# A six-layer perceiver block on one core: constant rows, background units, first keys and the last expert's rows are placed elsewhere

## What is computed

```
x = x + L0 linear cross-attention with ctx (4 x 2048 x 512)
x = x + L0 gated linear attention (128 steps), its output through Wo, plus the row bo
x = x + L0 feed-forward net 512 -> 2048 -> 512 (gelu), plus the row b2
x = x + L1 masked cross-attention with ctx, 16 heads
x = x + L1 causal self-attention with rotary embedding, 16 heads
x = x + L1 mixture of 8 experts, 2 per token (silu(x W1) * (x W3)) W2
```

## Time and profile before

| | |
|---|---|
| median of 3 runs | 1844.7 us (1841.14 to 1847.6) |
| the profiled execution | 1843.16 us |
| its span, first to last instruction | 1841.6 us |
| mean granted TensorE clock | 0.977 of 2.4 GHz |
| busy: PE, DVE, ACT, POOL | 94%, 64%, 53%, 13% |
| instructions | 25720 |

### The profile page before, as it was taken

The page is one execution under the profiler, slowest core; times in us unless marked ns, Lnnn a source line. Parts: engine busy times, 40 slices in busy tenths (PEclk is TensorE's granted clock), DMA queues, the critical chain, the costliest instruction groups (busy, mean ns, idle before and its releaser), DMA issues. The chain is left out here.

```text
span 1841.6 us, 25720 instructions
## 1 busy us (share of the span) xinstructions
PE 1740.0 (94%) x9446; PEld 1428.0 (78%) x9446; DVE 1172.4 (64%) x2453; ACT 982.1 (53%) x2033; POOL 235.9 (13%) x138
## 2 busy tenths in 40 slices
PE   7999999999898989999999999999899879999996
PEld 5778888877787779999899989887455557778785
DVE  5777777764534236667677767998434456785753
ACT  6676666642343235556566656887332345665552
POOL 0000000000000022112111211222111022221221
PEclk9999999999999999999999999999899979999998
DMA  6322222217400599778677867667500347786721
GB/s 227 119 104 86 98 81 102 69 69 286 166 1 23 183 290 301 240 225 248 188 234 220 245 188 221 178 197 246 198 6 7 119 165 249 248 299 208 275 65 59
DMA packets 147131, 310.01 MB, mean 168 GB/s; under 512 B 11472, under 2 KB 100816, under 8 KB 135440
## 3 DMA queue, kind: packets, MB, share of 16 engines
q1 hardware_dynamic: 145072, 301.85, 50.1%
q0 software_dynamic: 1920, 6.36, 1.1%
HBM read 226.88 MB, written 81.28 MB: 167 GB/s over the span
## 5 line engine op out<-in xcount | busy, mean ns | idle before, releaser
L1131 ACT CAST PTH<-bank 128x512 fp32r<-128x512 f32 x256 | 149.8, 585 | 164.9 <-PE bank L1126 164.9
L1133 DVE TENSOR_TENSOR PTL<-bank,PTH 128x512 fp32r<-128x512 f32 x256 | 176.0, 687 | 94.9 <-ACT PTH L1131 93.8
L1652 DVE TENSOR_TENSOR WS<-EW,WS 128x1024 fp32r<-128x1024 f32 (+1 forms) x120 | 148.4, 1244 | 80.9 <-ACT WS L1649 78.9
L1111 ACT ACTIVATE TT<-TT,MX 128x512 f32<-128x512 f32 x256 | 186.5, 729 | 8.6 <-DVE MX L1101 8.6
L1083 DVE CUSTOM_DVE_ANT_0 TT<-bank,MASK 128x512 f32<-128x512 f32 x256 | 174.1, 681 | 5.9 <-POOL MASK L1064 5.3
L1649 ACT CAST WS<-EW 128x1024 fp32r<-128x1024 f32 (+1 forms) x144 | 139.1, 977 | 63.3 <-PE bank L1669 62.5
L1126 PE MATMUL bank<-IDN,TT 128*128 128x128 f32 x1024 | 155.2, 274 | 4.0 <-DVE RS L1176 2.9
L101 PE MATMUL bank<-BCH,WKT 128*128 128x256 f32 x512 | 150.6, 294 | 5.2 <-DVE BCL L633 4.4
L102 PE MATMUL bank<-BCL,WKT 128*128 128x256 f32 x512 | 146.9, 287 | 0.0
L103 PE MATMUL bank<-BCH,WKT 128*128 128x256 f32 x512 | 146.8, 287 | 0.0
L1152 PE MATMUL bank<-PTH,VG 128*128 128x256 f32 x512 | 142.6, 300 | 0.2 <-DVE PTL L1133 0.2
(11 more groups left out here) (293 smaller groups left out, 4352.0 us busy)
## 6 DMA issues: line engine op xcount, KB each, us to landing
EW<-in_ewg SPq DMA_DIRECT2D x48, 1024.0 KB, 5.5
KST<-tmp_k SPq DMA_DIRECT2D x43, 768.0 KB, 5.7
tmp_k<-EKH SPq DMA_DIRECT2D x128, 256.0 KB, 2.8
EW<-in_ewg SPq DMA_DIRECT2D x24, 768.0 KB, 4.8
CT<-in_ctxT SPq DMA_DIRECT2D x32, 512.0 KB, 3.2
CN<-in_ctxN SPq DMA_DIRECT2D x32, 512.0 KB, 3.2
BCT<-in_ctxT SPq DMA_DIRECT2D x32, 512.0 KB, 3.5
tmp_k<-EKL SPq DMA_DIRECT2D x64, 256.0 KB, 2.7
```

Of the source, the lines that this page charges most:

```text
L1111: t_e[(n, kc)] = tick("act", act.activation(TT[:, sl, cs], TT[:, sl, cs], ACT.Exp, bias=MX[:, n % 4, 5:6], scale=SC1, accum_out=SUM[:, b % ...
L1131: t = tick("act", act.copy(PTH[:, q], bank[bk][:]))
L1133: t = free[bk] = tick("dve", dve.tensor_tensor(PTL[:, q], bank[bk][:], f(PTH[:, q]), ALU.subtract))
L1652: t_lo = tick(low, E[low].tensor_tensor(WS[:, s, 1, 0:n * w], src, f(WS[:, s, 0, 0:n * w]), ALU.subtract))
```

## The change

Four edits. (1) `GBO` is added to X of batch b in level b of the gated attention, and `B2R` in step 4 + b of the feed-forward loop. (2) At the end of both layers, the addition of a bank to X, `norm_rate`, and for batches 1 and 2 `norm_rows` of the batch before, stand together in `add_and_rate`, with one unit after each batch; `layernorm_all` begins with the transposes and loses its `bg(4)`. Before the feed-forward net it stands behind the split of the first weights. Before the cross-attention only SP waits ahead of it, and for the work up to the last feed-forward product; ACT and DVE wait for that behind it. (3) The units of batch 0 ahead of the first loads end with its last key tile (`k_done`); `load_head` waits for the keys' stores alone, and the four units left are issued after `load_head(0)`. (4) The last expert's rows are not stored. The selection matrices of its two blocks are turned (`ST`), the higher expert's rows of the other experts are gathered in the last expert behind `LB`, and X + `LB` + `HB` is written into four banks that a product has opened; then the rows' high and low halves (`YH`, `YL`) are added in those banks by products with `ST`. ACT and DVE copy the banks to X, and each batch is stored at once. The count for long lists is loaded in the last expert. The block for lists over 256 tokens makes its own gathers and additions and stores again; it is skipped with these inputs. In the diff the additions of `LB` stand behind the first block's eighth weight group, `open_sum` ahead of the second block's ninth, and `spread_one` is eight products that need the second block's halves and the four opened banks.

```diff
-        def layernorm_all(bg, high=None):
-            t_r = [norm_rate(b) for b in range(4)]
-            t_n = [norm_rows(b, t_r[b]) for b in range(2)] + [None] * 2
-            bg(4)
+        def add_and_rate(b, bk, t_r, t_n):
+            t = tick("dve", dve.tensor_tensor(X[:, b, :], X[:, b, :], bank[bk][:], ALU.add))
+            x_tok[b] = free[bk] = t
+            t_r[b] = norm_rate(b)
+            if 0 < b < 3:
+                t_n[b - 1] = norm_rows(b - 1, t_r[b - 1])
+        def add_row(b, row):
+            need("dve", x_tok[b])
+            x_tok[b] = tick("dve", dve.tensor_tensor(X[:, b, :], X[:, b, :], row, ALU.add))
+        def layernorm_all(bg, t_r, t_n, high=None):
...
+                    if c == 1 and g % 8 == 7:
+                        k_done[b] = list(bgs["kw"])
...
+            if 0 <= lev < 4:
+                add_row(lev, GBO[:])
             bg(2)
...
         for b in range(4):
             need("pe", free[4 + b])
-            t = tick("pe", pe.matmul(bank[4 + b][:], ..., GWO[:], start=True, stop=True))
-            need("dve", t, x_tok[b])
-            t = tick("dve", dve.tensor_tensor(X[:, b, :], X[:, b, :], bank[4 + b][:], ALU.add))
-            free[4 + b] = t
-            need("dve", t)
-            x_tok[b] = tick("dve", dve.tensor_tensor(X[:, b, :], X[:, b, :], GBO[:], ALU.add))
+            t_o.append(tick("pe", pe.matmul(bank[4 + b][:], ..., GWO[:], start=True, stop=True)))
+        for b in range(4):
+            need("dve", t_o[b], x_tok[b])
+            add_and_rate(b, 4 + b, t_r, t_n)
+            bg(1)
...
-        t_yt = layernorm_all(bg, YTH)
...
         split_w1(0)
+        t_yt = layernorm_all(bg, t_r, t_n, YTH)
...
+                if 4 <= i < 8:
+                    add_row(i - 4, B2R[:])
+        fg = so_far()
         for b in range(4):
             need("dve", t_y, x_tok[b])
-            t = tick("dve", dve.tensor_tensor(X[:, b, :], X[:, b, :], bank[4 + b][:], ALU.add))
...
-            x_tok[b] = tick("dve", dve.tensor_tensor(X[:, b, :], X[:, b, :], B2R[:], ALU.add))
+            add_and_rate(b, 4 + b, t_r, t_n)
+            bg(1)
...
-        fg = so_far()
-        for e in ("sp", "act", "dve"):
+        need("sp", *fg)
+        t_yt = layernorm_all(bg, t_r, t_n)
+        for e in ("act", "dve"):
             need(e, *fg)
-        t_yt = layernorm_all(bg)
         bg(2)
...
-        bg_rest()
+        while k_done[0] is None:
+            bg()
...
-                while kv_done[b] is None:
+                while k_done[b] is None:
                     bg()
-                need("sp", *kv_done[b])
+                need("sp", *k_done[b])
...
-        for n in range(NK):
+        load_head(0)
+        bg_rest()
+        for n in range(1, NK):
             load_head(n)
...
+        def out_high(v, bk):
+            T[v]["yh"] = tick(SEM[v]["act"], act.copy(YH[v][:], bank[bk][:]))
+        def out_low(v, bk):
+            T[v]["yl"] = tick(SEM[v]["dve"], dve.tensor_tensor(YL[v][:], bank[bk][:], f(YH[v][:]), ALU.subtract))
+        def turn_list(v):
+            need("pe", free[5], t_c)
+            for i in range(4):
+                m = pe.transpose(bank[5][:, 128 * i:128 * i + 128], f(GS[v][:, i, :]), IDN[:])
...
+            t_st[v] = free[5] = tick("act", act.copy(ST[v][:], bank[5][:].rearrange("p (a b) -> p a b", a=4)))
+        def open_sum(i, bk):
+            need("pe", free[bk], *t_st)
+            t = tick("pe", pe.matmul(bank[bk][:], ST[0][:, i, :], XG[0][:, 0], start=True, stop=True))
+            need("dve", t, t_hb[3], x_tok[i])
+            t_sum[i] = tick("dve", dve.tensor_tensor(bank[bk][:], X[:, i, :], HB[i], ALU.add))
+        def spread(v, i, bk, x, stop):
+            return pe.matmul(bank[bk][:], ST[v][:, i, :], (YH, YL)[x][v][:], start=False, stop=stop, skip_group_check=True)
...
                 if g == 1 and last:
                     for i in range(4):
                         back(i)
+                    for i in range(4):
+                        back_high(i)
+                    for eng in engines:
+                        load_count(eng, 8)
+                if g in (2, 3) and last:
+                    turn_list(g - 2)
...
+            if last:
+                for i in range(4):
+                    need("dve", t_lb[3])
+                    x_tok[i] = tick("dve", dve.tensor_tensor(X[:, i, :], X[:, i, :], LB[i], ALU.add))
...
+            sums = (b, b1, 4, 5)
+            if last:
+                for i in range(4):
+                    open_sum(i, sums[i])
...
+        when("pe", 7, spread_one)
+        out_high(0, a)
+        out_low(0, a)
+        need("pe", T[0]["yh"], *t_sum)
+        for i in range(4):
+            spread(0, i, sums[i], 0, False)
+        need("pe", T[0]["yl"])
+        for i in range(4):
+            t = tick("pe", spread(0, i, sums[i], 1, True))
+            e = ("act", "dve")[i % 2]
+            need(e, t)
+            x_tok[i] = tick(e, (dve.tensor_copy if i % 2 else act.copy)(X[:, i, :], bank[sums[i]][:]))
+            need("sp", x_tok[i])
+            t_out = dma("sp", "out", out[:, i], X[:, i])
...
-        for i in range(4):
-            t = tick("hb", pool.indirect_dma_start(HB[i][:], None, YD, ...))
-        for i in range(4):
-            need("dve", t_lb[3])
-            x_tok[i] = tick("dve", dve.tensor_tensor(X[:, i, :], X[:, i, :], LB[i][:], ALU.add))
-        for i in range(4):
-            need("dve", t_hb, x_tok[i])
-            x_tok[i] = tick("dve", dve.tensor_tensor(X[:, i, :], X[:, i, :], HB[i][:], ALU.add))
-        finish_at(stop)
+        need("sp", t_out, *so_far())
```

More of the change, by code:

```diff
@@ L612, in build @@
         kv_done = [None] * 4
+        k_done = [None] * 4
         def split_weights(dst, src, t):
@@ L1792, in group_one @@
                 when("dve", e, lambda: gate(1, g // 2, bk), ("dve1",))
-            if g == 8:
+            if g == 8 and e < 7:
                 when("act", e, lambda: out_act(1, bk), ("act1",))
                 store(e, 1)
+            if g == 8 and e == 7:
+                when("act", e, lambda: out_high(1, bk), ("act1",))
+                when("dve", e, lambda: out_low(1, bk), ("dve1",))
         def half_zero(e, g, h, bk):
@@ L1925, in build, with spread_one @@
             nxt = half_zero(e, 8, 1, a)
-            out_act(0, a)
-            store(e, 0)
+            if not last:
+                out_act(0, a)
+                store(e, 0)
             split_half(nxt)
-        engines = ("sp", "pe", "act", "dve", "pool")
+        def spread_one():
+            need("pe", T[1]["yh"], T[1]["yl"], *t_sum)
+            for i in range(4):
+                spread(1, i, sums[i], 0, False)
+                spread(1, i, sums[i], 1, False)
+        when("pe", 7, spread_one)
[5 more added lines that the diff above has]
+        need("pe", T[0]["yl"])
+        for i in range(4):
+            t = tick("pe", spread(0, i, sums[i], 1, True))
[4 more added lines that the diff above has]
+            t_out = dma("sp", "out", out[:, i], X[:, i])
         own = {"xsp0": "sp", "xsp1": "sp", "xpe": "pe", "xact": "act", "xdve": "dve"}
@@ L2034, in far_block @@
                 wait(eng, *[(o, P.count[o]) for o in own])
-        fin = [(k, P.count[k]) for k in ("pe", "act", "dve", "pool", "pe1", "peg", "act1", "dve1", "yw0", "yw1", "lb")]
+        fin = [(k, P.count[k]) for k in ("pe", "act", "dve", "pool", "pe1", "peg", "act1", "dve1", "yw0", "yw1", "lb",
+                                         "hb", "out")]
         blocks = {}
@@ L2044, in build, with far_add @@
                 blocks[e, kb] = todo, {o: P.count[o] - before[o] for o in own}
+        FAR = CMP[:, 0, 0:32].rearrange("p (a b) -> p a b", a=4)
+        XF, LF = P.sem_of("xfar"), P.sem_of("xlb")
+        def far_add():
+            steps = [
+                lambda: dve.tensor_scalar(FAR, POS[:], 256.0, None, ALU.is_ge),
+                lambda: dve.tensor_tensor(FAR, FAR, KEY[:], ALU.mult),
+                lambda: dve.tensor_reduce(KFT[:, 0:4], FAR, AX.X, ALU.add),
+                lambda: dve.tensor_reduce(KFT[:, 4:8], FAR, AX.X, ALU.max),
+                lambda: dve.tensor_tensor(KFT[:, 0:4], KFT[:, 0:4], KFT[:, 4:8], ALU.subtract),
+                lambda: dve.tensor_scalar(SM2[:], KFT[:, 0:8], 0.0, None, ALU.is_equal),
+                lambda: dve.tensor_scalar(SM2[:], SM2[:], 3585.0, None, ALU.mult),
+                lambda: dve.tensor_tensor(KFT[:, 0:8], KFT[:, 0:8], SM2[:], ALU.add),
+                lambda: dve.tensor_scalar(FIN[:], KFT[:, 0:8], -1.0, None, ALU.add)]
+            for n, step in enumerate(steps):
+                step().then_inc(XF, 1)
+                dve.wait_ge(XF, n + 1)
+            dve.wait_ge(LF, 128)
+            n = len(steps)
+            for rows in (LB, HB):
+                for i in range(4):
+                    dve.tensor_tensor(X[:, i, :], X[:, i, :], rows[i], ALU.add).then_inc(XF, 1)
+                    n += 1
+                dve.wait_ge(XF, n)
         for eng in engines:
-            need(eng, *fin)
```

(3 more changed lines are left out.)

45 lines of the change are left out of this document (32 added, 13 removed).

## The result

The changed kernel takes **1827.1 us**, the median of 4 runs (1825.0 to 1828.1), beside 1844.4 for the kernel before: a ratio of 0.9906, with a 95% interval of 0.9893 to 0.9919, so 17.3 us less (15 to 20). A second set of runs gave 1825.7 and 0.9903 (0.9889 to 0.9916). The forecast was 1821, a gain of 23.7 on the median shown then; 1827 lies in its range.

What follows compares the result with a forecast made beforehand. TensorE, busy for 94% of the span, was taken as the bound, so only its waits counted. Gains 6.5+4.8-1.1+3.9+8.3 = 22.4 us off the profiled 1843.2 gave 1820.8, stated as 1821, range 1814 to 1829.

Steps and rivals of the forecast that it cites:

- The constant rows: Eight additions (`GBO`, `B2R`), each as long as 0.69 us, leave the chains at both joins for beside products; cost nothing.
- Join 1: Between gated attention and feed-forward net: first feed-forward product 4.7 us sooner, 1.8 less low clock, sum 6.5; 1.4 gap remains.
- The walk: Step-by-step VectorE and TensorE timing between gated attention and feed-forward net: a 1.4 us gap remains, first feed-forward product at 491.5.
- Join 2: After the feed-forward net, up to the query products: gain 4.8 us, with a gap of 1.3 us remaining.
- The two gaps left: Gaps of 1.4 and 1.3 us remaining in the joins: clock charged behind one of the two, 1.1 us.
- Head 0's keys: Before the first score: key load goes out sooner, the gap and its low clock go, 3.9 us (ends 0 and 3.9).
- keys no sooner: Rival before the first score: the load's data come as late as now, gain there 0; 1825 us, chance 0.13.
- the forecast's own signs of being wrong: A gap over 3 us in any join, clock falling where 1.00 now, or TensorE waiting for a last-expert POOL split.
- The tail: Behind the last product: store, four gathers and eight additions removed, products added; 8.3 us gained (ends 5.5 and 10.1).
- The sum: Whole kernel: 6.5+4.8-1.1+3.9+8.3 = 22.4 us off the profiled execution of 1843.2, so 1820.8; forecast 1821.
- The slower rival: Background units: group 9's load goes 4 us late and later loads stay late, 3.8 us each; 1855 us, chance 0.04.

Runs made afterwards that it cites:

- the third better version: Changed kernel with head 2's loads later, last products ordered by batch, rows 2 and 3 ahead of `YTL`, first-join transposes in banks 4 to 7: 1821.6 us, 0.9889.
- the one with outputs by batch: Changed kernel with the last eight products ordered by batch (high and low of each batch together), not all highs first: 1826.0 us, 0.9908.

## Why the prediction was right, and where it was not

- **The constant rows**: right, nothing beside products (89.15 and 32.93 or 32.94 with and without).
- **Join 1**: 6.5 forecast. J1 went from 22.33 to 17.48 (forecast 17.6 for this distance) and FFN lost 1.5 of low clock (1.8 said): 6.3. The walk also had the place and length of the remaining gap, 1.58 for 1.4, between the second and the third transposes.
- **Join 2**: 4.8 forecast, 5.1 measured; gap 1.73 for 1.3.
- **The two gaps left**: 1.1 charged for the clock at one of them; it fell at neither (1.00 in both windows, and in the 4.0 us between the first gap and its window). By the rule of the Trainium skill's "TensorE: Matmul & The Clock Gate" that the forecast weighed, both would have been charged; these two windows do not bear it out.
- **Head 0's keys**: wrong. Of the sum's 3.9 nothing was left (0.8 lost). The load did go out sooner, landed under the units, and the first score comes 2.8 sooner than with the keys undone. The sum stops there. What failed is its answer to what is late next: it names the mask, and as moved only "group 9's load and the last value store". Batch 1's key stores stand behind the loads of three heads, the queries and the mask, and their buffer `EKH` holds up the next units. They stand there in the kernel before too, and ACT waits for them 12.23 us; but TensorE, which had itself been held for 2.64 us at the first score, does not run out of products. ACT, then the window around the end of its wait, in the kernel before:

```profile
683.06 0.59 ACT L655 CAST EKH<-bank 128x512 fp32r<-128x512 f32 x1 [12.23 <-DMA tmp_k<-EKH]
...
681.00:692.00 11.00, 11.00 (x66) 9.70 (x65) 6.79 (x18) 8.91 (x20) 5.33 (x1) 1.00 1.08 365
```

 The first score starts 17.6 us sooner in the changed kernel (672.85 to 655.22), ACT's wait ends only 15.7 sooner (683.06 to 667.37), and the lost time came back 10 us behind the first score. The rival "keys no sooner" gave the right sum for another reason. Two of the forecast's own signs of being wrong came with it: a gap over 3 us, and a clock that fell (0.64) where it was 1.00.
- **The tail**: 8.3 forecast, 5.8 by two profiles of each kernel (T 17.46 to 9.88, less the last expert's 1.8). The work ahead of the last weight product was right: over the last expert's products the windows give 97.67 and 99.46 us at clock 1.00 (1.8 said). The gathers fitted on POOL too, 1.26 us each, with 2.08 left where 1.6 was said:

```profile
L1929 POOL DMA_INDIRECT EW<-tmp_yd,FIN x4 | 5.0, 1261 | 1.2 <-issue 1.2
...
L1679 POOL TENSOR_TENSOR WS<-EW,WS 128x768 fp32r<-128x768 f32 x1 | 1.8, 1841 | 2.1 <-ACT WS L1676 2.1
```

 The terms as listed add up to an end at 1832.8, not the 1833.3 that was written; the forecast goes by the latter. The missed size is "the output's issue and its landing, 2.2": the last store lands 4.3 us after its issue, and 4.0 to 4.7 in all eleven profiles with the new tail, where the three with the old one have 2.3 at most. The four issues are not much closer together than they were: before, changed, and the third better version, which took longer over them than the kernel before and whose last store still lands in 4.3.

```profile
1837.49 2.14 SPq L62 DMA_DIRECT2D out<-X  x4
```

```profile
1820.91 1.96 SPq L62 DMA_DIRECT2D out<-X  x4
```

```profile
1813.43 2.28 SPq L62 DMA_DIRECT2D out<-X  x4
```

 What else differs is that loads of instructions stand among the stores' packets in the changed kernel (queue: packets, MB, share of the data engines, 1820.9 to 1826.8), and none in the kernel before (1837.4 to 1841.7):

```profile
q1 hardware_dynamic: 576, 1.05, 49.2%
q14 instruction: 5, 0.04, 1.9%
q8 instruction: 1, 0.02, 1.0%
```

```profile
q1 hardware_dynamic: 576, 1.05, 65.6%
```

 That these loads hold up the last store is not shown: no run moves them. The cause of the 4.3 stays open.
- **The sum**: 22.4 was forecast; by stages it is 6.3 + 5.1 + 0 + 0.9 + 5.8 = 18.1, where 0.9 is Q and S9 together, 77.98 to 77.10 in the mean of two profiles each; most of it is the clock behind the late group load, which fell in both profiles of before and in two of the twelve others, so not the keys'. The medians say 17.3 and 18.2. Single profiles differ by less (1841.2 to 1825.6 in the mean, 15.7), mostly by the self-attention, 4.5 longer there. That 1827 lies in the range rests on the joins and the rows, which were right in mechanism and size, and on the range's width: the keys and the tail fell short by 3.0 and 2.5, and the clock charge of 1.1 that did not come made up for part of it by luck.
- **The slower rival** (group loads late for good) did not come: that load costs 2.47 and is late once behind the joins, as before.

## What to carry to other kernels

When a wait for a load is removed, go on to the next wait in the same queue: list every transfer that follows until the queue is empty again, the stores of the next stage above all, and ask which buffer each one frees, also where it costs nothing yet. Where the data engines were already at 1.0, the wait removed at one transfer came back at the next, and moving bytes to later helped. A transfer's landing time read in one place isn't its price in another: the same four stores landed in 2.1 to 2.3 us in the kernel before and in 2.6 to 4.3 in the changed one.

## What the runs showed of the hardware

SP's issue of a store takes 0.36 to 0.50 us in the earlier trace rows, and up to 2.9 us in the changed kernel (659.63 above), where stores land in a median of 9.0. Full data engines alone don't do it: behind the first scores of the kernel before they are at 1.00, and the stores from `EKH` issued from 674 to 681 us take 0.43 to 0.60 us to issue, and land in 6.0 us in the median:

```profile
DMA to landing us min/median/max: 5.6/6.0/6.1
```

So a queue that is backed up for longer shows in the length of its issues. The clock behind gaps of nearly one length differs: it fell behind 2.19, 2.46 and 3.23 us, not behind 1.58 and 1.73, in one of two cases behind 1.6, and behind the late group load's 2.5 to 2.6 it fell in four of fourteen profiles. The Trainium skill's "TensorE: Matmul & The Clock Gate", What's actually happening, says that the point at which the clock changes varies from run to run; the self-attention of one and the same kernel, 190.06 and 188.62, agrees. In steps, too: its lengths in fourteen profiles are five values (184.0, 185.6 or 185.7, 187.7, 188.6, 190.0 or 190.1) and not a spread, and the changed kernel and the one with outputs by batch share the same one to 0.02 us.
